# Attention inside a transformer layer: row maxima in units of one psum bank of 512 keys, and two key blocks in three bunches of scores and maxima

## What is computed

```python
Q, K, V = heads(x @ Wq.T + bq), heads(x @ Wk.T + bk), heads(x @ Wv.T + bv)   # B, 16, 2048, 16
scores = einsum('bhqd,bhkd->bhqk', Q, K) / sqrt(16)
A = softmax(scores, axis=-1)
A_stable = 0.6 * A + 0.4 * L[None, None]       # L: a fixed band of 7 diagonals
out = einsum('bhqk,bhkd->bhqd', A_stable, V)
return out.reshape(B, S, 256) @ Wo.T + bo
```

## Time and profile before

| | us |
|---|---|
| median of 3 runs | 1961.0 (1960.85 to 1962.22) |
| the profiled execution | 1960.27 |
| its span in the profile | 1958.5 |
| PE busy / DVE busy / ACT busy / POOL busy | 1910.8 / 1638.5 / 1341.7 / 371.8 |
| granted TensorE clock over the span | 0.996 |

### The profile page before, as it was taken

How to read it: one execution, slowest core, us unless ns; L and a number is a source line. 1 busy time by engine, 2 the same in 40 slices (tenths; PEclk the granted TensorE clock), 3 DMA queues, 4 the chain that set the end, 5 groups by cost and what they waited for, 6 DMA issues and landing times. The chain is left out here.

```text
span 1958.5 us, 40904 instructions
## 1 busy us (share of the span) xinstructions
PE 1910.8 (98%) x16092; PEld 1007.8 (51%) x16092; DVE 1638.5 (84%) x2123; ACT 1341.7 (69%) x2390; POOL 371.8 (19%) x380
## 2 busy tenths in 40 slices
PE   7999999999999999999999999999998999999997
PEld 3543333333333333333333333334587799999997
DVE  6799999999999999999999999995277765555554
ACT  3348888888888888888888888888544422223232
POOL 1362110011101010011001100101035522313133
PEclk9999999999999999999999999999999999999999
DMA  7954556544564556545554555453235877778884
GB/s 266 253 106 86 96 103 113 101 88 111 107 107 89 110 100 108 94 87 116 110 100 88 111 109 105 89 111 73 90 126 186 287 242 234 237 251 274 273 259 115
DMA packets 132013, 279.58 MB, mean 143 GB/s; under 512 B 41696, under 2 KB 72416, under 8 KB 125152
## 3 DMA queue, kind: packets, MB, share of 16 engines
q1 hardware_dynamic: 118672, 259.17, 53.2%
q0 software_dynamic: 13152, 17.83, 4.7%
HBM read 215.93 MB, written 79.06 MB: 151 GB/s over the span
## 5 line engine op out<-in xcount | busy, mean ns | idle before, releaser
L676 DVE TENSOR_REDUCE part_max<-psum 128x1 f32<-128x1024 f32 x1024 | 1243.7, 1220 | 19.0 <-PE psum L779 14.0
L737 ACT ACTIVATE probs<-psum 128x512 f32<-128x512 f32 x2048 | 1111.0, 596 | 153.9 <-PE psum L789 115.4
L789 PE MATMUL psum<-score_q,score_k 50*128 50x512 f32 x2048 | 741.5, 444 | 0.0
L779 PE MATMUL psum<-max_k,max_q 48*128 48x512 f32 x2048 | 732.7, 446 | 1.0 <-DVE part_max L676 1.0
L801 PE MATMUL psum<-probs,v_ones 128*32 128x256 f32 x8192 | 654.1, 391 | 9.6 <-ACT heads_sb L743 9.2
L789 PEld LDWEIGHTS psum<-score_q,score_k 50*128 50x128 f32 x2048 | 304.5, 185 | 420.9 <-ACT probs L737 372.2
L801 PEld LDWEIGHTS psum<-probs,v_ones 128*32 128x32 f32 x8192 | 162.1, 107 | 378.5 <-ACT probs L737 194.2
L779 PEld LDWEIGHTS psum<-max_k,max_q 48*128 48x128 f32 x2048 | 294.4, 185 | 13.4 <-issue 7.0
L1201 ACT ACTIVATE x_sb<-psum,x_sb 128x512 f32<-128x512 f32 (+1 forms) x160 | 101.6, 636 | 259.6 <-PE psum L1572 257.1
L1591 PE MATMUL psum<-w,h_hi 128*128 128x256 f32 x1120 | 208.4, 282 | 0.6 <-DVE h_lo L1391 0.3
L1591 PEld LDWEIGHTS psum<-w,h_hi 128*128 128x128 f32 x1120 | 180.4, 188 | 11.9 <-DVE h_lo L1391 1.0
(11 more groups left out here) (177 smaller groups left out, 1239.7 us busy)
## 6 DMA issues: line engine op xcount, KB each, us to landing
w<-w_split SPq DMA_DIRECT2D x40, 2048.0 KB, 8.3
max_q<-qk_pieces SPq DMA_DIRECT2D x192, 128.0 KB, 7.0
score_k<-qk_pieces SPq DMA_DIRECT2D x192, 128.0 KB, 4.5
xs<-in_pads SPq DMA_DIRECT2D x33, 528.0 KB, 4.6
qk_pieces<-pieces SPq DMA_DIRECT2D x32, 512.0 KB, 4.7
w_split<-w_pair SPq DMA_DIRECT2D x32, 512.0 KB, 5.3
max_k<-qk_pieces SPq DMA_DIRECT2D x192, 64.0 KB, 7.6
score_q<-qk_pieces SPq DMA_DIRECT2D x192, 64.0 KB, 2.3
```

The source lines that it names most:

```text
L676: nc.vector.tensor_reduce(part_max[:, u, t, p:p + 1], ps_m[p].rearrange("q b f -> q (b f)"), axis=AXIS.X, op=ALU.max).then_inc(m_read, 1)
L737: nc.scalar.activation(probs[:, kb % PROBS, chunk * BLOCK:(chunk + 1) * BLOCK], bank_of(k, kb, c), ACT.Exp, scale=float(HD) ** -0.5).then_ ...
L779: last = nc.tensor.matmul(ps_m[p][:, h, :], max_q[u][rows, t * P:(t + 1) * P], max_k[u][rows, p * BLOCK:(p + 1) * BLOCK], start=True, stop ...
L789: nc.tensor.matmul(bank_of(k, kb, c), score_k[u][rows, kb * P:(kb + 1) * P], score_q[u][rows, part * BLOCK:(part + 1) * BLOCK], start=True ...
```

## The change

The maxima's unit becomes one bank: each of the four matmuls of a block of queries raises `m_ready`, DVE takes four maxima of 512 columns in place of two of 1024, `part_max` has four columns per block, and PE waits for the read four units back. The counts in the waits on `m_ready` and `m_read` go from `2 * ST` to `4 * ST`.

On PE, `body` gives way to three functions that each issue the next score, the next maximum or the next part of values, with their waits, and to a loop over double key blocks that calls them in three bunches: four matmuls, a part of values; six matmuls, two parts; six matmuls, one part. Two more scores are issued ahead of the loop (`SCORES_AHEAD`), so scores run two units further ahead of the values. The row tiles alternate so that each bunch still splits into pairs of h = 0 and h = 1. On ACT, `copy_o` comes one exponential later, behind the first one of the next head's kb = 1.

```diff
-                sp.wait_ge(m_ready, 2 * ST * (n + 1))
+                sp.wait_ge(m_ready, 4 * ST * (n + 1))
...
-            for p in range(2):
-                if p == 1 and between is not None:
+            for q in range(4):
+                if q == 2 and between is not None:
                     between()
-                dve.wait_ge(m_ready, 2 * g + p + 1)
-                nc.vector.tensor_reduce(part_max[:, u, t, p:p + 1], ps_m[p].rearrange("q b f -> q (b f)"),
+                dve.wait_ge(m_ready, 4 * g + q + 1)
+                nc.vector.tensor_reduce(part_max[:, u, t, q:q + 1], ps_m[q // 2][:, 1 - q % 2, :],
                                         axis=AXIS.X, op=ALU.max).then_inc(m_read, 1)
...
                     if not (last and kb == ST - 1):
                         exp(*nxt, c)
-                if kb == ST - 1:
-                    copy_o(n, k)
+                    if kb == 0 and c == 0 and n > 0:
+                        copy_o(n - 1, k - 1)
+            if last:
+                copy_o(n, k)
...
+        def maxima(g, t, u, q):
+
+            p, h = q // 2, 1 - q % 2
+            if g > 0:
+                pe.wait_ge(m_read, 4 * g + q - 3)
+            rows = slice(h * ROW_TILE, h * ROW_TILE + STACK)
+            nc.tensor.matmul(ps_m[p][:, h, :], max_q[u][rows, t * P:(t + 1) * P],
+                             max_k[u][rows, p * BLOCK:(p + 1) * BLOCK], start=True, stop=True).then_inc(m_ready, 1)
...
+        at = {"score": CH, "maximum": LOOK * 4, "values": 0}
...
+        for _ in range(SCORES_AHEAD):
+            score()
+        for _ in range(NHEADS * ST // 2):
+            score()
+            maximum()
+            score()
+            maximum()
+            value()
+            maximum()
+            maximum()
+            score()
+            score()
+            score()
+            maximum()
+            value()
+            value()
+            maximum()
+            score()
+            score()
+            maximum()
+            score()
+            maximum()
+            value()
```

More of the change, by code:

```diff
@@ L50 @@
 INVERT_AT = 4
+SCORES_AHEAD = 2
 FIRST_LOCAL, FIRST_HEADS = (1, 2), (7, 8, 9, 10)
@@ L830, in _ @@
                 half = 2 * t + p
-                maxima(t, t % ST, t // ST, p)
+                maxima(t, t % ST, t // ST, 2 * p)
+                maxima(t, t % ST, t // ST, 2 * p + 1)
                 if half == FIRST_SCORES:
@@ L840, in _ @@
         pe.wait_ge(v_copied, BANKS)
[L842 to L881, removed]
@@ L883, in _, with score @@
-        by_head(body)
+        at = {"score": CH, "maximum": LOOK * 4, "values": 0}
+        def score():
+            unit = at["score"]
+            at["score"] += 1
+            if unit >= NHEADS * UNITS:
+                return
+            n, kb, c = unit // UNITS, unit % UNITS // CH, unit % CH
+            if kb == 0 and c == 0:
+                pe.wait_ge(score_in[n % 2], 16 * STACK_DMAS * (n // 2 + 1))
+                pe.wait_ge(shift_in[n % 2], 16 * SHIFT_DMAS * (n // 2 + 1))
+            scores(n, n, kb, c)
@@ new lines, in maximum, with value @@
+        def maximum():
+            unit = at["maximum"]
+            at["maximum"] += 1
+            g, part = unit // 4, unit % 4
+            if g >= NHEADS * ST:
+                return
+            m = g // ST
+            if g % ST == 0 and part == 0:
+                pe.wait_ge(max_in[m % 2], 16 * STACK_DMAS * (m // 2 if m % 2 == 0 else m // 2 + 1))
+            maxima(g, g % ST, m % 2, part)
+        def value():
+            n, kb, part = at["values"] // (PARTS * ST), at["values"] // PARTS % ST, at["values"] % PARTS
+            at["values"] += 1
+            if kb == 0 and part == 0:
+                pe.wait_ge(v_in, n + 1)
+            values(n, kb, n % 2, part)
+            if n == NHEADS - 1 and part == PARTS - 1:
+                fill(kb)
@@ new lines, in fill @@
+        def fill(kb):
+            if kb in FIRST_LOCAL:
+                m = FIRST_LOCAL.index(kb)
+                pe.wait_ge(keep["band_in"], 16)
+                pe.wait_ge(m_read, 4 * ST * NHEADS)
+                local_values(nc, keep, psum[:, 4 + m, :], 0, m).then_inc(keep["a_ready"][m], 1)
+            if kb in FIRST_HEADS:
+                t = FIRST_HEADS.index(kb)
+                for m in range(KD):
+                    pe.wait_ge(keep["a_copied"][m], 1)
+                done = project_heads(nc, keep, ps_m[1], t)
+                if t == BT - 1:
+                    done.then_inc(keep["o_ready"], 1)
@@ L1686, in program @@
                 keep["bias_v"] = head_sb("bias_v", [P, DIM])
-                for n, shape, dt in (("part_max", [P, 2, ST, 2], F32), ("neg_max", [P, ST], F32),
+                for n, shape, dt in (("part_max", [P, 2, ST, 4], F32), ("neg_max", [P, ST], F32),
                                      ("shift", [P, PIECES, ST], F32R), ("shift_tok", [P, PIECES * ST], F32)):
```

2 lines of the change are left out of this document (1 added, 1 removed).

## The result

The changed kernel takes 1936.4 us (median of 4 runs, 1934.6 to 1938.9) against 1961.4 for the kernel before on the same chip: a ratio of 0.9874, with a 95% interval of 0.9861 to 0.9886, so 1.3% faster. The forecast was 1935 in a range of 1900 to 1958. The profiled execution took 1934.6 us, its span 1932.8. Of the six executions of the kernel with the earlier shift, further down, one ran at a mean granted clock of 0.849 and took 2004.0 us; its median and ratio leave that one out.

What follows compares the result with a forecast made beforehand. PE was taken to bound the kernel before, DVE 7% behind. From 1960.3 us, -30 + 2 + 1.5 + 1 = -25.5 gave 1934.8; the median runs 0.7 above, so 1935, with 1900 to 1958 as the 8-in-10 range.

Steps and rivals of the forecast that it cites:

- PE is the bound: Attention in the kernel before: PE sets the pace at 1.23 us per half key block, DVE only 7% behind.
- PE's 4.62 for 4.92.: PE in attention: three bunches for four take 4.62 us per double key block for 4.92, saving 0.30.
- ACT would show as a bound if both others came below 4.4: ACT in attention: its exponentials and copies need 4.39 us per double key block, so it binds only under 4.4.
- faster than that: Rival, chance 0.10: a 512-wide maximum costs 0.57 us, PE and the shift's chain decide: 1911 us, 1890 without the chain.
- 0.599 us from start to start.: DVE: one 512-wide maximum costs 1.137 - 0.538 = 0.599 us from start to start; bounds 0.57 and 0.69.
- The rival that adds up whole durations: Rival, chance 0.15: short maxima on DVE don't overlap and cost 0.682 us each: 2104 us.
- DVE becomes the bound: DVE in attention needs 4.84 us per double key block, more than PE's 4.62, so it sets the pace.
- The -30 for the window: Main stretch of attention: 246 double key blocks at 4.84 us for 4.96 save 30 us.
- the shift's +2: Next head's first score waits for the shift's way through memory; late heads up to 0.4 us late: +2 us.
- The rival of the shift: Rival, chance 0.20: the shift's way back takes 36.2 us in all heads, so a head takes 39.5: 1955 us.
- The ring feeds DVE without a gap.: Banks between PE and DVE: reads starting 0.1 to 0.7 us in neither starve nor block PE; no idle added.
- With PE ahead of DVE this pays nothing: ACT's copy of the head's output, one exponential later: values' wait, 9.2 us in all, mostly goes, but gains nothing.

Runs made afterwards that it cites:

- the earlier shift: The second half paired, plus LOOK 22, SHIFT_AT 10, POOL splitting the shift before scaling the head, SP sending it before storing the head: 1918.8 us, ratio 0.9780.
- the run with mixed units: Changed kernel, but DVE reads two banks in one instruction wherever both matmuls lie in one bunch, the others singly: 1990.9 us, ratio 1.0139.
- the units alone: Kernel before with one-bank units of 512 columns for the maxima, old order on PE: 1965.1 us, ratio 1.0005.
- the shift late: Changed kernel with the transpose of the shift two key blocks later (SHIFT_AT 13 for 11): 2101.0 us in one execution.
- short maxima: Changed kernel with each maximum reading 448 of its 512 columns: 1921.8 us in one execution, ratio 0.9787.
- short exponentials: Changed kernel with maxima reading 448 of 512 columns and each exponential handling 384 of its 512 queries: 1901.3 us in one execution.
- the second half paired: Changed kernel, but of each block of queries DVE reads the first two banks singly, the last two in one instruction: 1922.5 us, ratio 0.9803.

## Why the prediction was right

**"PE is the bound" of the kernel before.** Right, and shown: 11% less work on DVE changed nothing in the old order.

**"PE's 4.62 for 4.92."** Right for the steps that it was made of: 4.59 where nothing else holds PE. But with ACT at its own length PE needs 4.70, and 38.09 / 8 = 4.76 with its share of the copy. The term left out was the third score in a row against a ring of three banks. "ACT would show as a bound if both others came below 4.4" was too low for that reason: it holds PE up by 0.11 although in the changed kernel it is busy only 1038 of 1196 us. The rival "faster than that", priced at 1911, came out near 1922 when the maxima were made shorter still.

**"0.599 us from start to start."** Right: 0.595 to 0.601. The two rows that made it, an operation's slope between 512 and 1024 columns and the 0.08 us that back-to-back instructions overlap, carried over to a shape that was not in the trace. The rival that adds up whole durations (2104) fell at once, and so did what the Trainium skill ("VectorE: DVE Perf Modes", the section on the DRAIN) would make of it: by an estimate from that rule and the trace's durations, 64 maxima of 0.68 with nothing under each other would be 43.5 us per head, and the heads take 38.84.

**"DVE becomes the bound", 4.84 per double block.** Right: 4.86, copies 38.84 apart. The -30 for the window was -25.6 with what stood for the shift's +2 in it, so the saving itself was sized some 3 us too large: a head takes 38.84, and 8 x 4.84 is 38.7. Three heads were longer in the profiled execution (copies 39.26, 39.13 and 39.44 apart), 1.3 us in all; in the first and the last of them the shift's load came 3.9 and 4.5 after its store, where it comes 2.8 after it in most. The middle one has no late load and stays unexplained. The rival of the shift was priced with a chain of 36.2; the two rows beside it give 35.8 and 33.7, so 39.1 per head at most by them.

**"The ring feeds DVE without a gap."** Right for this kernel, and for a reason that the forecast gave only half of: its window of starts says when DVE is fed, and the run with mixed units showed that it has to be asked at the point where PE waits. The same layout used for that run was wrong by 94 us.

**"With PE ahead of DVE this pays nothing"**, of the copy's move. This is the weak step. For the change as it stands no wait was left to cost, and the total came out right. But the sentence says that the old place would have done as well, and it costs 15 us. The stall was counted where it stood before, in front of values, with its 9.2 us in all; with the scores two units further ahead it would have come back in front of the scores, three times as long. So the size of the whole was right while the shares of its parts were not known, and in how close it came there is luck. The forecast's arithmetic had one number for a change with four parts that need each other: all but the one-bank units 2096, the units alone 1965, all but the copy's move 1952, all but the scores ahead 2068, all of it 1936.

**The sides.** +1.5 for the first maxima was +1.1, +1 for the end was +0.0. The terms of attention come to -24.5 for the -25.5 forecast, and 1.2 us that the untouched stages happened to be shorter in that execution bring the total to -25.7. That the forecast met the median within 1.4 us, where the four executions spread over 4.3, is luck.

## What to carry to other kernels

Where two engines are within a few per cent, cost each one's stream by start-to-start distances in stretches in which it has work in hand; durations overlap, and a wait can hide in a busy time. To see whether a ring feeds an engine, stand at the point where the producer is let go, add up the reads that the consumer still holds then, and compare that with the producer's time to its next delivery: reads in smaller pieces can pay for their overhead, and pairing those that free nothing urgent takes most of it back. Cost a moved step at the place where it stood, under the new order of everything else, before calling the move free.

## What the runs showed of the hardware

One instruction over two psum banks with two results (128 x 2 from 128 x 1024) takes 1212 ns, no longer than one with a single result (1220 before). Less the overlap of 0.08 that is 1.13 for two singles of 0.60, so pairing saves 0.07.

With the shift late, PE stood for 2.9 to 4.0 us once in each head, and behind it its clock was granted at half speed for 3.4 or 6.8 us. In all other runs it was 1.00 from 200 to 1300 us, with two exceptions of 3.4 us each: at 1085.0 with short maxima, behind a stand of 0.97 us, and at 1180.5 with short exponentials, behind one of 1.37. In these two runs stands of 1.03 and of 1.89 us left the clock as it was, and so did 0.4 us in every double key block with no scores ahead. So the length of one stand doesn't tell whether the clock falls; what does is open.

Open: why in some heads the shift's load is issued 3.7 to 5.0 us after its store, where it is 2.7 to 2.9 in most. In the kernel before it was so in all heads from the copy at 844.62 on the earlier trace rows, in the changed kernel in two, with the short maxima and with the second half paired in most of the later ones, with the earlier shift in two. No run separated what else was in the queues then.
